# A graph network with a mixture of experts: the second product of a tile behind the first of the next, and the routing's exponentials first

## The chip, the cores and the metric

The kernel runs on one core of one Trainium2 chip. Its time is that of one execution on the device, in microseconds (us); of several runs the median counts. The engines are named as the profile names them: PE (TensorE, its weight loads apart as PEld), DVE (VectorE), ACT (ScalarE), POOL (GpSimd) and SP (SyncE), which here only issues DMAs.

## The reference

Four layers follow each other on 3125 nodes with 256 numbers each, each behind a layer norm and added to its input: a graph convolution over 50,000 edges, an attention over slices, a second, two-step graph convolution with PReLU, and a mixture of eight experts. Only the last one matters here:

```python
def _L1_ffn_ref(x, gate_w, gate_b, W1, b1, W2, b2):
    xf = x.reshape(-1, Dd)
    probs = jax.nn.softmax(xf @ gate_w + gate_b, axis=-1)
    top2_vals, top2_idx = jax.lax.top_k(probs, 2)
    cw = zeros((N, Ee)).at[arange(N)[:, None], top2_idx].add(top2_vals)
    def step(acc, params):
        w1, bb1, w2, bb2, we = params
        h = jax.nn.gelu(xf @ w1 + bb1, approximate=False)
        y = h @ w2 + bb2
        return (acc + we[:, None] * y, None)
    out, _ = jax.lax.scan(step, jnp.zeros_like(xf), (W1, b1, W2, b2, cw.T))
```

w1 is 256 x 512 and w2 512 x 256 for each expert, all in float32. Each node needs only its two chosen experts.

## The kernel before

The kernel is written without a scheduler: each engine has its own list of instructions, and semaphores order them across engines. What matters lies in the last block, the experts (from line 1985). There the rows that go to the same expert are collected into tiles. There are 39 of them (TILES). The first 13 (FULL = 13) are narrow, 128 rows each, and their plan is made from the first 1280 nodes only, so that they can begin early. The other 26 are planned from all nodes by a longer computation; of them two wide tiles of 256 rows are followed by one narrow tile, over and over, and tile 38 is narrow too. So tiles 13, 14, 16, 17, 19, 20 and so on are wide.

A tile n goes through these steps:

- POOL gathers its rows from memory, an indirect DMA for each 128 rows, together with their gates (gather, line 1966, recorded at 1967). There are four buffers for the rows of a tile, eight for the narrow tiles at the start.
- PE transposes the rows (turn, line 2346, recorded at 2353) into bank n % 2. This waits for the gather.
- The transposes are copied out of the bank (take): for tiles 0 to 12 by ACT (line 2246, recorded at 2250), from tile 13 on by DVE (line 2090, recorded at 2094).
- PE makes the first product (hidden, line 2357, recorded at 2365), in two halves into two banks. It waits for the copy and for the first weights of the tile's expert, which SP loads (512 KB, line 2544) into one of two buffers when the first product of tile n-2 is done.
- ACT applies the bias and the Gelu in four instructions (line 2333), after the second product of tile n-2 has let go of their buffer.
- PE makes the second product (line 2500); all second weights are in SBUF. In the texts it is called y(n).
- DVE adds the second bias and multiplies by the gate of each row (evict, line 2096, recorded at 2105 and 2108).
- POOL adds the result to the output in memory, by an indirect DMA with accumulation for each 128 rows (line 2615). The scatter of tile n waits until that of tile n-1 has landed, since two tiles can hold the same row.

The order of each engine is written out by hand. PE has turn(0), hidden(0), and then for each n hidden(n) (where n > 0), turn(n+1) and the second product of n (lines 2474 to 2503). ACT has for each n its four activations, then take(n+1); for n = 0 then the exponentials of the routing (lines 2322 to 2342), for which DVE waits at 2122. Exponential and Gelu need different tables in ACT, each of which is loaded when it isn't there. DVE interleaves the routing of all nodes with the evictions of tiles 0 to 9 (lines 2113 to 2236). Of this routing: the choices are ready at 2140 (e_dv 2), the gates at 2141 (e_dv 3); PE then sums the choices for tile 3 (line 2490) and their ranks ahead of the second product of tile 4 (line 2492), DVE copies the ranks at 2161; the one-hots of the places are at 2218 to 2223, and PE multiplies them at line 2468, ahead of the second product of tile 10; from that DVE makes the table of rows (line 2232, e_dv 6). From tile 10 on DVE has, for each n, take(n+1) (where n+1 is at least 13) and evict(n).

POOL (lines 2601 to 2621) waits for evict(n), then gathers: tile n+8 as long as that is under 13; tile n+4 for n = 9 to 12, ahead of the scatter of n, where n = 9 waits for the table of rows; and for n from 13 on tile n+4 behind the scatters of n. SP (lines 2537 to 2555) stores all rows and gates (1980 KB) between the weight loads of tiles 4 and 5, when the gates are ready.

Of the kernel before, what the change touches and what calls it, by code (L numbers as in the profile page):

```python
# [7 lines left out]
ALU, ACT, AX = mybir.AluOpType, mybir.ActivationFunctionType, mybir.AxisListType  # L8
# [27 lines left out]
FULL = -(-(2 * CA * P - X * (P - 1)) // P)  # L36
# [4 lines left out]
TILES = FULL + REST  # L41
# [44 lines left out]
def build(nc, x, src, dst, g0_w, g0_b, w_fx, b_fx, w_x, b_x, w_slice, b_slice, w_q, w_k, w_v,  # L86
# [3 lines left out]
    with ctx:  # L90
# [1611 lines left out]
        def table(m, w=NC * X):  # L1702
            return SR[:, m * NC * X:m * NC * X + w]
        lg, prob, one1, one2, tmp, pick, rank, slot = (
            table(m).rearrange("p (c e) -> p c e", e=X) for m in range(8))
# [266 lines left out]
        def expert_of(eng, n):  # L1972
            if n < FULL:
                return eng.value_load(ftile_i[0:1, n:n + 1], min_val=0, max_val=X - 1)
            return eng.value_load(tile_i[0:1, numbered(n):numbered(n) + 1], min_val=0, max_val=X - 1)
# [9 lines left out]
        with nc.Block() as block:  # L1985
            @block.vector
            def _(dve):
# [102 lines left out]
                def take(n):  # L2090
                    dve.wait_ge(x_tr.sem, n + 1)
                    dve.wait_ge(h_mm.sem, 2 * (n - 1))
                    w = KF * parts(n) * P
                    nc.vector.tensor_copy(xT[:, n % 2, 0:w], ps[n % 2][:, 0:w]).then_inc(x_cp.sem, 1)
# [140 lines left out]
                step(nc.vector.tensor_tensor(out_f, out_f, row_f, ALU.add))  # L2235
                step(nc.vector.tensor_copy(out_i, out_f))
                for n in range(10, TILES):
                    if FULL <= n + 1 < TILES:
                        take(n + 1)
                    evict(n)  # L2240

                ch.close(step.done)

            @block.scalar
            def _(act):
                def take(n):
                    act.wait_ge(x_tr.sem, n + 1)
                    if n >= 2:
                        act.wait_ge(h_mm.sem, 2 * (n - 1))
                    nc.scalar.copy(xT[:, n % 2, 0:F], ps[n % 2][:, 0:F]).then_inc(x_cp.sem, 1)  # L2250
# [71 lines left out]
                for n in range(TILES):  # L2322
                    if n == FULL:
                        act.wait_ge(e_dv.sem, 4)
                    b = n % 2
                    w = parts(n) * P
                    expert = expert_of(act, n)
                    if n >= 2:
                        act.wait_ge(y_mm.sem, n - 1)
                    for m in range(KH):  # L2330
                        if m % 2 == 0:
                            act.wait_ge(h_mm.sem, 2 * n + m // 2 + 1)
                        last = nc.scalar.activation(hT[:, b, m, 0:w],  # L2333
                                                    ps[2 + 2 * b + m // 2][:, (m % 2) * w:(m % 2 + 1) * w], ACT.Gelu,
                                                    bias=b1T[:, bass.ds(expert, 1), m:m + 1].rearrange("p a k -> p (a k)"))
                        if m % 2:
                            last.then_inc(h_ac.sem, 1)
                    if n + 1 < FULL:
                        take(n + 1)
                    if n == 0:  # L2340
                        act.wait_ge(e_dv.sem, 1)
                        nc.scalar.activation(prob, lg, ACT.Exp).then_inc(e_ac.sem, 1)

            @block.tensor
            def _(pe):
# [125 lines left out]

                pe.wait_ge(e_ld.sem, e_ld.at(16 * (KH + 1 + X)))

                for n in range(TILES):
                    b = n % 2
                    expert = expert_of(pe, n)

                    if n:
                        hidden(n)

                    if n + 1 < TILES:
                        turn(n + 1)

                    if n == 0:
                        pe.wait_ge(e_dv.sem, 1)
                    if n >= 2:
                        pe.wait_ge(y_ev.sem, n - 1)
                    if n == 3:
                        pe.wait_ge(e_dv.sem, 2)
                        nc.tensor.matmul(ps[7][:, F:F + NC * X], ones[:], picks, start=True, stop=True)  # L2490
                    if n == 4:
                        nc.tensor.matmul(ps[6][:, F:F + NC * X], before[:], picks, start=True, stop=True)
                    if n == 10:
                        places_of(0)
                        places_of(1)
                    for h in range(parts(n)):
                        for k in range(KH):
                            if h == 0 and k % 2 == 0:
                                pe.wait_ge(h_ac.sem, 2 * n + k // 2 + 1)
                            last = nc.tensor.matmul(ps[6 + b][:, h * F:(h + 1) * F], hT[:, b, k, h * P:(h + 1) * P],  # L2500
                                                    w2[:, k, bass.ds(expert, 1), :].rearrange("p a n -> p (a n)"),
                                                    start=(k == 0), stop=(k == KH - 1))
                    last.then_inc(y_mm.sem, 1)

            @block.sync
            def _(sp):
# [137 lines left out]
```

## Time and profile before

| what | us |
|---|---|
| median of 3 runs | 1302.27 |
| the three runs | 1302.27, 1302.09, 1312.83 |
| span of the profiled execution | 1300.2 |
| PE busy in it | 1227.5 |
| POOL busy in it | 200.3 |

The profiled execution's whole time isn't given apart from its span; by the median some 2.1 us lie around the span. The experts take the last quarter of it, from about 1050 us on. PE's rows in a timeline begin before the end of the row ahead, as matmuls are pipelined; the rows of the chain have this taken off. "<-" in a row names what ended the idle time in front of it. A float32 product is recorded as two matmuls, so that a first or second product of one tile has 16 records (8 for the second product of a narrow tile).

### The profile page before, as it was taken

What the parts mean: (1) busy time and instruction counts of PE and PEld (TensorE: products, weight loads), DVE (VectorE), ACT (ScalarE), POOL (GpSimd) and SP (SyncE); (2) the same over time, 40 slices, a digit from 0 to 9 for tenths busy, and PEclk for the clock granted to TensorE, in tenths of its full rate; (3) what the DMA queues carried; (4) which work ended last, traced back from release to release, by engine and by line L of the source; (5) the groups of instructions that cost most, each with busy time, mean ns of one, the idle gap of its engine ahead of it and who ended that gap; (6) DMA issues with size and microseconds to landing.
All of it is one profiled execution on the core that took longest, in us unless ns stands there. A gap on an engine that the chain in (4) does not pass through costs nothing.

```text
span 1300.2 us, 20280 instructions
## 1 busy us (share of the span) xinstructions
PE 1227.5 (94%) x7475; PEld 843.3 (65%) x7475; DVE 580.9 (45%) x1601; ACT 488.8 (38%) x1192; POOL 200.3 (15%) x205
## 2 busy tenths in 40 slices
PE   3599999989999999999999999999999989899996
PEld 2377777745557644457777644447777778788885
DVE  5968877567764511221333332231224656323231
ACT  5865666357743597760000000110212243222221
POOL 3000000023310000000000000000000043577664
PEclk8599999999999999999999999999999989999998
DMA  6133123310003055566556445569766657566663
GB/s 190 30 128 104 49 103 128 135 38 1 1 1 129 2 176 152 153 152 152 127 127 127 127 142 153 154 148 210 163 118 122 193 176 205 136 160 150 148 148 66
DMA packets 256968, 159.96 MB, mean 123 GB/s; under 512 B 172832, under 2 KB 243951, under 8 KB 256732
## 3 DMA queue, kind: packets, MB, share of 16 engines
q1 hardware_dynamic: 245788, 143.58, 40.2%
q0 software_dynamic: 11072, 14.97, 6.5%
q8 instruction: 64, 1.05, 0.3%
q14 instruction: 44, 0.36, 0.1%
HBM read 82.15 MB, written 36.35 MB: 91 GB/s over the span
## 4 chain that ended last, share of the span: by engine, by line
PE 61%; DVE 3%; DMA 3%; issue 1%; POOL 0%; ACT 0%; POOLq 0%; DVEq 0%; ACTq 0%
PE bank L1010 21%; PE bank L1024 21%; PE bank L2500 7%; PE bank L2365 6%; PE bank L1045 2%; PE bank L1655 2%; DMA out<-weights,first_places 2%; PE bank L2353 1%; PE bank L1907 1%; DVE bnbuf L824 0%; PE bank L1897 0%; DVE weights L2058 0%; DMA normed<-rows_and_gates,agg_in_out 0%; DVE tb L2023 0%; DMA out<-weights,agg_in_out 0%
## 5 line engine op out<-in xcount | busy, mean ns | idle before, releaser
L1010 PE MATMUL bank<-weights,agg_in_out 128*128 128x320 f16 x2000 | 274.8, 299 | 0.0
L1024 PE MATMUL bank<-weights 128*128 128x512 f16 x1250 | 271.1, 379 | 0.9 <-issue 0.8
L1010 PEld LDWEIGHTS bank<-weights,agg_in_out 128*128 128x128 f16 x2000 | 195.7, 98 | 76.2
L1024 PEld LDWEIGHTS bank<-weights 128*128 128x128 f16 x1250 | 121.8, 98 | 149.5 <-DVEq L2015 2.1
L1147 PE MATMUL bank<-weights,agg_in_out 128*128 128x320 f16 x1000 | 163.1, 299 | 1.6 <-ACT weights L543 1.6
L543 ACT CAST weights<-bank 128x500 f16<-128x500 f32 x160 | 114.1, 723 | 66.9 <-PE bank L532 66.9
L840 POOL TENSOR_TENSOR shift<-shift,rstd 128x5 f32<-128x5 f32 x15 | 3.7, 245 | 865.1 <-ACT rstd L845 865.1
L2333 ACT ACTIVATE weights<-bank,weights 128x128 f32<-128x128 f32 (+1 forms) x156 | 55.8, 411 | 163.1 <-PE bank L2365 125.5
L2500 PE MATMUL bank<-weights 128*128 x448 | 111.2, 396 | 3.0 <-ACT weights L2333 2.8
L1147 PEld LDWEIGHTS bank<-weights,agg_in_out 128*128 128x128 f16 x1000 | 91.6, 98 | 28.5 <-issue 2.3
L2365 PE MATMUL bank<-wk,weights 128*128 128x128 f32 (+1 forms) x624 | 106.6, 325 | 2.9 <-DMA weights<-in_L_ffn_W 2.7
L2013 DVE SCALAR_TENSOR_TENSOR wk<-bank,inverse_degree,wk 128x256 f32<-128x256 f32 x50 | 24.0, 480 | 182.2 <-ACT wk L2271 182.2
L2365 PEld LDWEIGHTS bank<-wk,weights 128*128 128x128 f32 x624 | 96.3, 196 | 12.7 <-DMA weights<-in_L_ffn_W 3.1
L2500 PEld LDWEIGHTS bank<-weights 128*128 128x128 f32 x448 | 83.2, 196 | 20.0 <-issue 10.3
L1055 ACT COPY agg_in_out<-bank 128x320 f32<-128x320 f32 x20 | 8.5, 427 | 213.7 <-PE bank L1010 213.7
L2271 ACT ACTIVATE wk<-bank,inverse_degree 128x256 f32<-128x256 f32 x50 | 23.6, 474 | 153.0 <-PE bank L1024 142.2
L522 DVE TENSOR_TENSOR wk<-iota,low_source 128x512 f16<-128x512 f16 x160 | 67.4, 421 | 28.6 <-PE bank L532 26.8
L532 PE MATMUL bank<-wn,wk 128*128 128x125 f16 x640 | 64.5, 227 | 13.7 <-DVE wn L523 12.6
L2615 POOL DMA_INDIRECT out<-weights,agg_in_out x43 | 68.4, 1590 | 42.4 <-DMA out<-weights,agg_in_out 23.9
L1063 DVE COPY agg_in_out<-bank 128x320 f32<-128x320 f32 x20 | 9.8, 491 | 140.1 <-PE bank L1010 120.1
L532 PEld LDWEIGHTS bank<-wn,wk 128*128 128x128 f16 x640 | 49.4, 101 | 29.2 <-DVE wn L523 17.3
L523 DVE TENSOR_TENSOR wn<-iota_quarters,row_of_edge 128x504 f16<-128x504 f16 x160 | 66.5, 416 | 0.0
(428 smaller groups left out, 1465.9 us busy)
## 6 DMA issues: line engine op xcount, KB each, us to landing
weights<-counts_source_target SPq DMA_DIRECT2D x50, 800.0 KB, 4.6
counts_source_target<-weights SPq DMA_DIRECT2D x5, 4000.0 KB, 14.0
weights<-in_L_ffn_W SPq DMA_DIRECT2D x39, 512.0 KB
weights<-in_L_ffn_W SPq DMA_DIRECT2D x4, 1024.0 KB, 5.6
residual<-in_x SPq DMA_DIRECT2D x4, 640.0 KB, 5.1
rows_and_gates<-normed SPq DMA_DIRECT2D x1, 1980.0 KB
out<-residual SPq DMA_DIRECT2D x1, 1792.0 KB
first_rows_and_gates<-normed SPq DMA_DIRECT2D x1, 1320.0 KB, 6.0
```

The costliest lines, as they stand in the source:

```text
L522: nc.vector.tensor_tensor(couples(ohs[:, u]), ramp(4, P), twins(slo2[:, g, :], P), ALU.is_equal)
L523: nc.vector.tensor_tensor(couples(ohr[:, u, :, 0:NR + 1]), quarter_ramp(4, NR + 1), twins(rk2[:, g, :], NR + 1), ALU.is_equal).then_inc(q_ ...
L532: last = nc.tensor.matmul(ps[QBANK[u]][:, t * NR:(t + 1) * NR], ohs[:, u, t, :], ohr[:, u, t, 0:NR], start=True, stop=True)
L543: nc.scalar.copy(to, ps[QBANK[q % 4]][:, 0:4 * NR].rearrange("p (t n c) -> p t c n", t=4, c=NC)).then_inc(q_ev.sem, 1)
L1010: last = nc.tensor.matmul(bank, source[:, 5 * k + c, part * F + fh * P:part * F + fh * P + P], MB[:, k, c, h * HALF:(h + 1) * HALF], start ...
L1024: last = nc.tensor.matmul(ps[j][:, :], MB[:, k, c, j * P:(j + 1) * P], source[:, 5 * k + c, :], start=(k == 0 and c == 0), stop=(k == 4 an ...
L1045: last = nc.tensor.matmul(ps[product_bank(n)][:, 0:F], aggT[:, k, c * P:(c + 1) * P], gw[:, kw, k, :], start=(k == 0), stop=(k == KF - 1))
L1147: last = nc.tensor.matmul(bank, XH2[:, c, part * F + fh * P:part * F + fh * P + P], ats[b % 2][:, c, h * HALF:(h + 1) * HALF], start=(m == ...
L2333: last = nc.scalar.activation(hT[:, b, m, 0:w], ps[2 + 2 * b + m // 2][:, (m % 2) * w:(m % 2 + 1) * w], ACT.Gelu, bias=b1T[:, bass.ds(expe ...
L2365: last = nc.tensor.matmul(ps[2 + 2 * b + m // 2][:, (m % 2) * w:(m % 2 + 1) * w], w1b[:, b, k, m * P:(m + 1) * P], xT[:, b, k * w:(k + 1) ...
L2500: last = nc.tensor.matmul(ps[6 + b][:, h * F:(h + 1) * F], hT[:, b, k, h * P:(h + 1) * P], w2[:, k, bass.ds(expert, 1), :].rearrange("p a ...
L2615: pool.indirect_dma_start(out=out, in_=results_at(n)[:, h, :], in_offset=None, out_offset=bass.IndirectOffsetOnAxis(ap=rows_of(n, h, out_i ...
```

## The change

On PE turn(1) comes first, and then for each n hidden(n+1), turn(n+2) and the second product of n. At the border (tile 12 to 13) this is taken back: hidden(13), turn(13) and turn(14) come behind the second product of tile 12, since tile 13 needs the plan of all nodes. On ACT the copy for tile 1 and the exponentials come first of all, and take(n+1) stands between the two halves of the activations of n for n = 1 to 11. On DVE take(n+2) comes ahead of evict(n) from n = 13 on; take(13) stands ahead of evict(12) and take(14) behind it. POOL and SP are as before.

```diff
@@ -2235,9 +2235,13 @@
                 for n in range(10, TILES):
-                    if FULL <= n + 1 < TILES:
-                        take(n + 1)
+                    if n == FULL - 1:
+                        take(FULL)
+                    if FULL + 2 <= n + 2 < TILES:
+                        take(n + 2)
                     evict(n)
+                    if n == FULL - 1:
+                        take(FULL + 1)
@@ -2325,9 +2329,15 @@
                     expert = expert_of(act, n)
+                    if n == 0:
+                        take(1)
+                        act.wait_ge(e_dv.sem, 1)
+                        nc.scalar.activation(prob, lg, ACT.Exp).then_inc(e_ac.sem, 1)
                     if n >= 2:
                         act.wait_ge(y_mm.sem, n - 1)
                     for m in range(KH):
+                        if m == 2 and 0 < n < FULL - 1:
+                            take(n + 1)
                         if m % 2 == 0:
                             act.wait_ge(h_mm.sem, 2 * n + m // 2 + 1)
...
-                    if n + 1 < FULL:
-                        take(n + 1)
-                    if n == 0:
-                        act.wait_ge(e_dv.sem, 1)
-                        nc.scalar.activation(prob, lg, ACT.Exp).then_inc(e_ac.sem, 1)
@@ -2471,15 +2476,15 @@
+                turn(1)
                 for n in range(TILES):
                     b = n % 2
                     expert = expert_of(pe, n)
 
-                    if n:
-                        hidden(n)
-
-                    if n + 1 < TILES:
-                        turn(n + 1)
+                    if n + 1 < TILES and n != FULL - 1:
+                        hidden(n + 1)
+                    if n + 2 < TILES and not FULL <= n + 2 <= FULL + 1:
+                        turn(n + 2)
@@ -2501,6 +2506,10 @@
                     last.then_inc(y_mm.sem, 1)
+                    if n == FULL - 1:
+                        turn(FULL)
+                        hidden(FULL)
+                        turn(FULL + 1)
```

## Rows read from the trace of the kernel before

**Rows 1.** The page, first part: busy us, share of span, instructions.

```profile
PE 1227.5 (94%) x7475; PEld 843.3 (65%) x7475; DVE 580.9 (45%) x1601; ACT 488.8 (38%) x1192; POOL 200.3 (15%) x205
```

**Rows 2.** Busy time by stretch; after the five engines: clock, DMA share, GB/s.

```profile
1050.00:1100.00 50.00, 44.17 (x269) 39.02 (x268) 25.14 (x95) 21.58 (x57) 18.28 (x18) 0.89 0.67 197
...
1200.00:1250.00 50.00, 49.94 (x257) 43.15 (x256) 13.91 (x30) 12.07 (x31) 35.23 (x27) 1.00 0.65 150
```

**Rows 3.** Chain of waits, one round: start us, length us, what.

```profile
1148.51 3.53 PE bank L2500 x16
1152.05 3.45 PE bank L2365 x16
1155.72 0.86 PE bank L2500 x4
1156.61 2.85 PE bank L2500 x12
1159.46 1.78 PE bank L2365 x16
1161.69 1.74 PE bank L2500 x8
...
1167.31 3.53 PE bank L2500 x16
```

**Rows 4.** Timelines of PE, ACT and DVE, tiles 0 and 1.

```profile
1058.74 3.77 PE L2500 MATMUL bank<-weights 128*128 x8 [1.53 <-ACT weights L2333]
...
1066.41 1.99 PE L2500 MATMUL bank<-weights 128*128 x8 [1.04 <-ACT weights L2333]
...
1059.29 1.28 ACT L2342 ACT_TABLE_LOAD   x1
...
1064.35 1.28 ACT L2333 ACT_TABLE_LOAD   x1 [3.39 <-PE bank L2365]
...
1068.57 0.42 DVE L2105 TENSOR_TENSOR weights<-bank,weights 128x256 f32<-128x256 f32 x1 [2.07 <-PE bank L2500]
```

**Rows 5.** Timelines of PE and DVE around tiles 4 and 5.

```profile
1079.08 1.89 PE L2500 MATMUL bank<-weights 128*128 x8
1083.67 2.91 PE L2365 MATMUL bank<-wk,weights 128*128 128x128 f32 x16 [2.69 <-DMA weights<-in_L_ffn_W]
...
1081.92 0.37 DVE L2161 COPY agg_in_out<-bank 128x200 f32<-128x200 f32 x1
...
1089.47 0.43 DVE L2105 TENSOR_TENSOR weights<-bank,weights 128x256 f32<-128x256 f32 x1 [2.53 <-PE bank L2500]
```

**Rows 6.** Tiles 12 to 14: timelines of PE and DVE, then chain of waits.

```profile
1121.73 0.71 PE L2353 MATMUL bank<-ident,normed 128*128 128x128 f32 x4 [2.11 <-DMA normed<-rows_and_gates,agg_in_out]
...
1129.73 0.69 DVE L2094 COPY wk<-bank 128x512 f32<-128x512 f32 x1 [2.84 <-PE bank L2353]
...
1116.88 4.81 DMA normed<-rows_and_gates,agg_in_out
...
1122.45 3.36 PE bank L2500 x8
```

**Rows 7.** Timeline of POOL behind tile 16's second product.

```profile
1154.61 1.62 POOL L2615 DMA_INDIRECT out<-weights,agg_in_out  x1 [0.30 <-issue]
...
1158.41 1.08 POOL L1967 DMA_INDIRECT normed<-rows_and_gates,agg_in_out  x1 [0.30 <-issue]
1159.80 1.05 POOL L1967 DMA_INDIRECT normed<-rows_and_gates,agg_in_out  x1 [0.30 <-issue]
```

**Rows 8.** Chain of waits, the end.

```profile
1287.94 3.79 DMA out<-weights,agg_in_out
```

**Rows 9.** DMA engines' busy tenths, 1151 to 1158 in 40 slices.

```profile
DMA  9940003100000057560000396420000029332997
```

**Rows 10.** Busy time by stretch around two gaps of PE.

```profile
1081.00:1089.00 8.00, 5.33 (x26) 4.96 (x27) 4.51 (x21) 1.52 (x5) 3.09 (x3) 0.79 0.70 210
...
1106.00:1114.00 8.00, 6.16 (x72) 5.77 (x71) 5.01 (x9) 1.51 (x5) 3.11 (x2) 1.00 0.42 124
```

## The prediction

> **What bounds the kernel now.** I read the page's first part, then the table by stretches, then the chain of waits from 1050 us on, then the timeline of each engine there. TensorE is busy for 94% of the span [rows 1], and the edit touches only what follows about 1057 us, so the question is how near to full the expert stage is and what fills the rest. Two stretches differ [rows 2]: from 1050 to 1100 TensorE is busy 44 of 50 us with VectorE at 25, from 1200 to 1250 it is busy 49.94 of 50.
>
> In the second stretch (tiles 13 to 38, in the pattern wide, wide, narrow) the chain is TensorE alone [rows 3]. A wide tile costs 3.45 us for the first product (x16, line 2365) and 3.53 for the second (line 2500), a narrow one 1.78 and 1.74. Between a first and a second product stand the transposes of the next tile: 0.22 us for two, 0.45 for four. From the end of tile 16's second product (1152.04) to the end of tile 19's (1170.84) one round of three tiles takes 18.8 us. Only one real wait is in it: the split into 0.86 + 2.85 of a second product behind a narrow tile's transposes, some 0.2 us late on the activations. The whole edit can take 0.2 us a round out of this stretch.
>
> In the first stretch (tiles 0 to 12, narrow) VectorE makes the routing tables between the evictions, and the gather of tile 13 waits for it. TensorE has three gaps there: 1.04 us ahead of tile 1's second product [rows 4], 2.69 us ahead of tile 5's first product, where the weights of tile 5 come behind the 1980 KB store of rows and gates [rows 5], and 2.1 us at tile 13's transposes, for its gather [rows 6].
>
> **The sum's base.** The profile's span is 1300.2 us and the median of the timed runs 1302.27, so 2.1 us lie around the span. Differences are worked out in the span and put on the median. A measurement of this kernel can tell about 1% (13 us) from no change.
>
> **Part 1, the exponentials ahead of tile 0's activations.** Before: Gelu table, four activations, a copy, a table load of 1.28 us, the exponential; then another load of 1.28 at tile 1 [rows 4]. After: copy, load, exponential, load, activations. One load of 1.28 us goes, and VectorE gets its exponentials about that much sooner. But tile 0's second product, which began at 1058.74, now has the copy, a load (1.28) and the exponential ahead of its activations, and the copy waits for tile 1's transposes: some 3 us later. Meanwhile TensorE does the first product of tile 1. VectorE then waits for tile 1's second product, which ended at 1068.24 and whose eviction at 1068.57 cost it 2.07 us of waiting [rows 4]. I put that product's end at 1068.6, so the 1.3 us are eaten and the routing goes on 0 to 0.5 us late. Bounds: 1.3 us sooner to 1.5 later. I take 0.3 later.
>
> **Part 2, the shifted order in tiles 1 to 12.** With weights in time the order changes nothing, as each activation gets more cover. The exception is tile 5. Its weights are queued on SP behind the store of rows and gates, which waits for VectorE's gates (about 1073), and land at 1083.6 whatever TensorE does. Before, the second product of tile 4 came ahead of this wait and ended at 1080.97; VectorE read its ranks at 1081.92 [rows 5]. Now hidden(5) and turn(6) (first product and transposes) stand ahead of y(4) (second product). TensorE runs dry after y(3), near 1077, and waits some 7 us instead of 2.7; then come the first product (2.9 us, at the lower clock, as in the row of before), transposes, ranks and y(4), ending at 89 to 90. VectorE's copy of the ranks moves from 1081.9 to about 1089.5. It had waited 2.53 us in front of tile 5's eviction at 1089.47 [rows 5], which it gets back in part: the 5.0 us of steps between copy and eviction start late, and evict(5) comes at about 1095.5. The routing is then 6 us late and stays so, since from there VectorE works without a wait for TensorE. Bounds: 4 us (if the gates come 1.3 us sooner) to 8.
>
> How much reaches tile 13? The second of its two gathers began at 1116.88 and landed 4.81 us later [rows 6]. Now it begins near 1123 and lands between 1126 and 1128, and turn(13) starts near 1127.4 instead of 1121.73. In return y(12), which took 3.36 us at the lower clock behind turn(13) before [rows 6], is now done ahead of it, for nothing. Before, hidden(13) began at 1125.8. Now it begins after turn(13) (0.45) and VectorE's copy (0.69 by the row of tile 14's [rows 6], with both hand-overs an estimated 0.95), at 1128.8, and hidden(14) waits for its own copy again, 0.95, as no second product stands between. Sum at the border: 3.0 + 0.95 = +4.0 us. Bounds: +1 (no delay of the routing) to +7.
>
> **Part 3, the wide stretch: the gather gets less time.** POOL's order is unchanged: after evict(n) it scatters tile n, then gathers tile n+4. Turn(n+4) needs that gather. Before, hidden(n+1) to hidden(n+3), y(n+1), y(n+2) and two turns lay between y(n) and turn(n+4). In the new order hidden(n+2), turn(n+3), y(n+1) and hidden(n+3) are all: one product of each kind and one turn less. Take tile 16 [rows 3, 7]: Its second product ended at 1152.04, its scatters began at 1154.61 (2.57 later: eviction by VectorE, semaphores, POOL just free), its two gathers for tile 20 ended on POOL at 1160.85. So 8.8 us pass before the gather is even sent. To land: the last scatter of the run landed 3.79 us after its start, of which POOL took 1.55, so 2.2 after [rows 8]; tile 13's gather 3.8 after, behind weight loads [rows 6]; and the DMA view of 1151 to 1158 shows the engines busy until about 1155.5 after the gather that POOL finished at 1154.3, so at least 1.2 [rows 9]. I take 2.1, nearest to the scatter's row and to the quiet view.
>
> Now the loop over one round: y(16) ends; 2.57 + 6.24 + 2.1 = 10.9 to the landing; turn(20) 0.45; y(18) 1.74; hidden(20) 3.45; turn(21) 0.22; y(19) 3.53. Sum 20.3 us, against 18.8 that TensorE needs now. The leg of TensorE in it is 9.4, so the gather would have to be there in 9.4 us and takes 10.9. TensorE waits 1.5 to 1.7 us before turn(17), 20, 23 and so on, once a round. The other two gathers of a round have room as soon as this one has stretched it. POOL's own work, 5 scatters at 1.9 and 5 gathers at 1.4 with the waits for landings, is near 17.9 and does not bind. From tile 17 to tile 38 there are 7 rounds: 7 x 1.5 = +10.5 us. Bounds by landing: 1.2 gives +4, 3.8 gives +22.
>
> The Trainium skill ("DMA: Bandwidth & Descriptors", Anatomy of one DMA — SWDGE (gpsimd) path) gives a fixed 2.0 us and the bytes over 436e3 a microsecond; for 128 rows of 264 floats that is an estimate of 2.3 us, and the loop would be 20.5 and the part +12. By the row of tile 13's gather it would be +22. No row of before shows a gather's landing in the quiet stretch.
>
> **Part 4, the tail.** The end is set by the scatters of tiles 37 and 38 behind y(37). Hidden(38) now stands ahead of y(37): +1.8 us.
>
> Sum: 4.0 + 10.5 + 1.8 = +16.3, thus 1302.3 + 16.3 = 1318.6; I say 1318.
>
> **Rivals.**
> A (0.5): the forecast, 1310 to 1324.
> B (0.2): the gather lands fast, 1.2 us after POOL, or the routing loses nothing. The loop is 19.4, 7 x 0.6 = +4, border +2 to 4, tail 1.8: about +9, 1310 or a little below. For it: the quiet view of rows 9. Against: the scatter's 2.2.
> C (0.2): the waits make the clock fall. Around the 2.7 us gap of tile 5 the mean granted clock was 0.79 and the next products took 2.9 instead of 2.0 us; around the 1.84 us gap at 1109 it stayed at 1.00 [rows 10]. A gap of 1.6 is below that, hence the small chance. A fall costs about 1.7 us (tile 12's product: 3.36 for 1.74), in the loop, 7 times: +12, 1330. The Trainium skill ("TensorE: Matmul & The Clock Gate", HAM oscillation — how this bites in real kernels) tells of kernels in which a wait in every pass throttles the array each time; by it the time would be this 1330.
> D (0.1): not slower. The scatters and gathers keep up: the landing is hidden because POOL starts earlier than 2.57 us after the product. It decides at 9.4 us from y(n) to the landing. Then the 0.2 us waits go (8 x 0.2), y(12) covers 1.7 of the gather's wait and the exponentials give 1.3: -4.6, 1298. Against: the 8.8 us already spent on POOL's rows leave 0.6 for a landing, and no row shows one so short. More than 1% faster would need 13 us, while all gaps of TensorE in the stage together are about 9.
>
> Chances: over 1% slower (above 1315.3) is most of A and all of C, 0.58; within 1% the rest of A, B and D, 0.38; faster by over 1% 0.04. Range 1304 to 1331.
>
> **What would show it.** Right: TensorE's row at line 2353 waits 1.5 us once a round "<- DMA normed"; busy in 1200 to 1250 falls from 49.9 to about 46; rounds of 20.3 us; a 7 us gap at line 2365 near 1077 to 1084; the eviction of tile 5 near 1095; two table loads after 1056 us instead of three. Wrong: rounds of 18.6 with no wait at line 2353; evict(5) still near 1089; or a granted clock below 0.95 in 1150 to 1250, which is rival C.

## The result: slower by 1.3%, and the profile after

The changed kernel takes 1324.38 us (median of 6 runs, 1323.08 to 1327.81) where the kernel before, run beside it, takes 1305.4 (6 runs, 1302.09 to 1312.83). The medians lie 19.0 us apart. The ratio is 1.0127, with a 95% interval of 1.0099 to 1.0156: slower by 1.0 to 1.6%, or 16.6 us by the ratio. I had forecast 1318, in a range of 1304 to 1331, with slower by over 1% at 0.58. The spans of the two profiled executions, 1300.2 and 1321.7 us, lie 21.5 us apart. That is more than the 16.6 us of the ratio, since the profiled execution of before was among its fastest.

The page of the changed kernel, its span and first part, has the work unchanged, against [rows 1]:

```profile
span 1321.7 us, 20280 instructions
...
PE 1225.7 (93%) x7475; PEld 844.7 (64%) x7475; DVE 581.7 (44%) x1601; ACT 486.8 (37%) x1191; POOL 200.1 (15%) x205
```

The table of busy time by stretch answers to [rows 2]:

```profile
1050.00:1100.00 50.00, 40.44 (x257) 37.69 (x257) 20.01 (x76) 18.70 (x52) 15.77 (x13) 0.85 0.67 191
...
1200.00:1250.00 50.00, 46.60 (x247) 40.27 (x246) 13.05 (x27) 12.13 (x32) 31.38 (x24) 1.00 0.58 137
```

TensorE, busy 49.94 us of the stretch from 1200 to 1250 before, has 46.60 now, with the clock still at 1.00. In the first stretch it falls from 44.17 to 40.44, and there the mean granted clock falls from 0.89 to 0.85 (its two levels are 2.4 and 1.2 GHz, 1.00 and 0.5). POOL, busy 35.23 us from 1200 on, has 31.38, the same work in longer rounds.

**The wide stretch.** The chain of waits of the changed kernel, one round from tile 16's second product to the transposes of tile 20, and on to those of tile 23 (start us, length us, what):

```profile
1160.75 3.47 PE bank L2505 x16
...
1166.65 0.36 POOL out L2624
...
1168.57 1.56 POOL out L2624
...
1170.44 1.07 POOL normed L1967
...
1171.82 3.41 DMA normed<-rows_and_gates,agg_in_out
1175.28 0.66 PE bank L2358 x4
1175.93 1.73 PE bank L2505 x8
1177.66 3.45 PE bank L2370 x16
...
1181.34 3.47 PE bank L2505 x16
...
1195.89 0.66 PE bank L2358 x4
```

In [rows 3] this was TensorE alone. Now the chain leaves it. The second product ends at 1164.22, two scatters start at 1166.65 and 1168.57, two gathers follow, the second of which starts at 1171.82, and 3.41 us later its rows are there, 2.4 after POOL is done with it. Only then do tile 20's transposes run, and behind them 1.73, 3.45, 0.22 and 3.47 us of TensorE. From 1175.28 to 1195.89 a round takes 20.6 us, where it took 18.8. From the product's end to the landing it is 11.0 us, and TensorE had work for 9.2 of them.

From 1216 us on the waits are mostly spread over two transposes of a round, 0.2 to 1.2 us each, and the chain also goes over landings of scatters. This one is tile 27's:

```profile
1241.93 6.08 DMA out<-weights,agg_in_out
```

Tile 28's scatters wait for it on POOL, and the gather of tile 32 stands behind them. The rounds stay at 20.0 to 20.9 us.

**Tiles 4 and 5.** The timelines of PE and DVE of the changed kernel, against [rows 5]:

```profile
1073.54 1.89 PE L2505 MATMUL bank<-weights 128*128 x8
1083.80 3.78 PE L2370 MATMUL bank<-wk,weights 128*128 128x128 f32 x16 [8.37 <-DMA weights<-in_L_ffn_W]
...
1088.46 2.18 PE L2505 MATMUL bank<-weights 128*128 x8
...
1090.74 0.37 DVE L2161 COPY agg_in_out<-bank 128x200 f32<-128x200 f32 x1 [9.97 <-PE bank L2505]
...
1096.87 0.42 DVE L2105 TENSOR_TENSOR weights<-bank,weights 128x256 f32<-128x256 f32 x1 [0.86 <-issue]
```

Tile 3's second product is done at 1075.4, then TensorE waits 8.37 us for tile 5's weights; the second product of tile 4 runs behind that, at 1088.46 instead of 1079.08. VectorE copies the ranks at 1090.74 instead of 1081.92 and evicts tile 5 at 1096.87 instead of 1089.47.

**The border.** The timeline of PE at tiles 13 and 14, against [rows 6]:

```profile
1128.95 0.66 PE L2358 MATMUL bank<-ident,normed 128*128 128x128 f32 x4 [2.09 <-DMA normed<-rows_and_gates,agg_in_out]
1130.43 5.16 PE L2370 MATMUL bank<-wk,weights 128*128 128x256 f32 x16 [0.83 <-issue]
...
1136.86 3.69 PE L2370 MATMUL bank<-wk,weights 128*128 128x256 f32 x16 [0.83 <-issue]
...
1140.61 3.62 PE L2505 MATMUL bank<-weights 128*128 x16
```

The transposes of tile 13 start 7.2 us later than before. Each of the two first products waits 0.83 us; VectorE's copy (0.69 us, the first from 1129.64 on) ends 0.1 us before the first of them starts. The first of them takes 5.16 us instead of 3.45 at full clock. When it and the second product of tile 13 and the first of tile 14 are done (1140.77 + 3.47 = 1144.24) the kernel before stood at 1136.90 (the start of tile 14's second product, behind 1133.23 + 3.45 + 0.22, in its chain).

### The profile page after: what moved, and what is told of

Its sections match the earlier page's. It is cut to its first block, busy times and chain, and to the rows that moved or that the text cites. A ratio compares the mean times of both kernels' runs of the same rounds, so it can differ in the third digit from the quotient of the medians.

```text
span 1321.7 us, 20280 instructions
## 1 busy us (share of the span) xinstructions
PE 1225.7 (93%) x7475; PEld 844.7 (64%) x7475; DVE 581.7 (44%) x1601; ACT 486.8 (37%) x1191; POOL 200.1 (15%) x205
## 4 chain that ended last, share of the span: by engine, by line
PE 53%; DVE 5%; DMA 4%; issue 4%; POOL 2%; DVEq 0%; POOLq 0%; ACT 0%; SPq 0%; ACTq 0%
PE bank L1010 21%; PE bank L1024 20%; PE bank L2505 3%; PE bank L2370 3%; PE bank L1045 2%; PE bank L1655 2%; DMA normed<-rows_and_gates,agg_in_out 2%; DMA out<-weights,agg_in_out 1%; POOL out L2624 1%; PE bank L1907 1%; DMA weights<-in_L_ffn_W 1%; POOL normed L1967 1%; DVE weights L2105 1%; PE bank L2358 1%; PE bank L1897 0%
## 5 line engine op out<-in xcount | busy, mean ns | idle before, releaser
L2370 PE MATMUL bank<-wk,weights 128*128 128x128 f32 (+1 forms) x624 | 110.3, 333 | 11.0 <-DMA weights<-in_L_ffn_W 8.4
L2370 PEld LDWEIGHTS bank<-wk,weights 128*128 128x128 f32 x624 | 99.4, 202 | 20.7 <-DMA weights<-in_L_ffn_W 8.8
L2505 PE MATMUL bank<-weights 128*128 x448 | 103.6, 381 | 1.1 <-DVE weights L2108 1.1
```

Source lines behind the costliest of these rows:

```text
L2370: last = nc.tensor.matmul(ps[2 + 2 * b + m // 2][:, (m % 2) * w:(m % 2 + 1) * w], w1b[:, b, k, m * P:(m + 1) * P], xT[:, b, k * w:(k + 1) ...
```

## The experiments

Ratios are to the kernel before, which ran beside each group on the same chip; its median was 1307 to 1309 us in those. The groups ran on different chips, so runs of two groups are compared by their ratios.

### The gathers ahead of the scatters

```diff
-                    if FULL <= n + 4 < FULL + 4:
+                    if FULL <= n + 4 < TILES:
                         gather(pool, n + 4)
...
-                    if FULL + 4 <= n + 4 < TILES:
-                        gather(pool, n + 4)
```

> The changed kernel with one edit on POOL: from tile 13 on the gather of tile n+4 comes ahead of the scatters of tile n instead of behind them, so it is sent some 3.8 us sooner; nothing else moves. My theory (the wide stretch loses because the gather of tile n+4 has 9.4 us where it takes 10.9 to 11.3): the loop over a round falls from 20.6 to under 18.6, TensorE's waits at the transposes in the wide stretch vanish, and the time falls by 10 to 13 us against the changed kernel, to 5 to 9 us above the kernel before. Rival 1 (the loss comes from VectorE's copies standing ahead of the evictions, or from the order on TensorE itself): the waits stay or move to the products and the time stays within 3 us of the changed kernel, 19 us above the one before. Rival 2 (POOL as a whole is the bound): nothing is gained either, as its sum of work is the same.

Measured: 1311.4 us, ratio 1.0038 [1.0015, 1.0062], so 5 us above the kernel before and 12 below the changed one by the ratios. In the first rounds the chain of waits of this run is TensorE's alone again:

```profile
1140.34 3.46 PE bank L2505 x16
1143.79 1.78 PE bank L2370 x16
...
1146.01 3.46 PE bank L2505 x16
1149.47 3.45 PE bank L2370 x16
...
1158.76 3.46 PE bank L2505 x16
```

From 1140.34 to 1158.76, wide tile to the same wide tile of the next round, it takes 18.4 us, 0.4 less than before: the product behind a narrow tile's transposes is in one piece of 3.46 us now, where [rows 3] had it split into 0.86 and 2.85. From 1125 us on TensorE's transposes wait for gathers 2.4 us in all, against 13.6 in the changed kernel. All the extra rounds' time hangs on when POOL sends the gather. The rivals fall: VectorE's copies and TensorE's order are as in the changed kernel, and so is the sum of POOL's work. What stays is the border: tile 13's second product ends at 1143.80, 6.9 us behind the same work before. From 1240 us on the chain goes over POOL's scatters and their landings, a bound that comes back below.

### Part 1 alone: the exponentials first

```diff
                     expert = expert_of(act, n)
+                    if n == 0:
+                        take(1)
+                        act.wait_ge(e_dv.sem, 1)
+                        nc.scalar.activation(prob, lg, ACT.Exp).then_inc(e_ac.sem, 1)
...
-                    if n + 1 < FULL:
+                    if 0 < n < FULL - 1:
                         take(n + 1)
-                    if n == 0:
-                        act.wait_ge(e_dv.sem, 1)
-                        nc.scalar.activation(prob, lg, ACT.Exp).then_inc(e_ac.sem, 1)
```

> The kernel before with part 1 alone: on ScalarE the copy for tile 1 and the exponentials stand ahead of tile 0's activations; TensorE, VectorE and POOL keep their old order. My theory (one table load goes, VectorE then waits for the second product of tile 1 anyway, so nothing of it arrives): within 2 us of the kernel before, the choices ready at 1072 to 1074 us. Rival (the routing's chain carries the gain through to tile 13's gather): 1.3 us or more faster, all later routing steps sooner by that much.

Measured: 1308.79 us, ratio 1.0012 [0.9988, 1.0037]: no difference. The timeline of DVE in this run:

```profile
1059.32 0.36 DVE L2122 TENSOR_REDUCE agg_in_out<-agg_in_out 128x25 f32<-128x200 f32 x1 [0.43 <-ACT agg_in_out L2331]
...
1065.49 0.42 DVE L2105 TENSOR_TENSOR weights<-bank,weights 128x256 f32<-128x256 f32 x1 [4.75 <-PE bank L2501]
...
1073.90 0.28 DVE L2141 TENSOR_TENSOR normed<-agg_in_out 128x120 f32<-128x120 f32 x1
```

The exponentials arrive at 1059.32 (1060.99 before). Then VectorE waits 4.75 us for tile 0's second product, evicts at 1065.49 what it evicted at 1063.28, and has the gates 1.1 us later than before (1073.90 against 1072.77). In the changed kernel the earlier exponentials look so, in the timelines of ACT and then DVE:

```profile
1058.30 0.37 ACT L2335 ACTIVATE agg_in_out<-agg_in_out 128x200 f32<-128x200 f32 x1 [0.16 <-DVE agg_in_out L2119]
1058.69 1.28 ACT L2343 ACT_TABLE_LOAD   x1
...
1064.13 0.42 DVE L2105 TENSOR_TENSOR weights<-bank,weights 128x256 f32<-128x256 f32 x1 [4.01 <-PE bank L2505]
...
1068.15 0.42 DVE L2105 TENSOR_TENSOR weights<-bank,weights 128x256 f32<-128x256 f32 x1 [0.80 <-PE bank L2505]
```

The exponential at 1058.30, one load behind it, evictions of tiles 0 and 1 at 1064.13 and 1068.15 against 1063.28 and 1068.57 [rows 4]: an even trade.

This run has the old order in the wide stretch, and yet its profile shows the transposes there waiting for gathers in three places (timeline of PE):

```profile
1149.40 0.65 PE L2354 MATMUL bank<-ident,normed 128*128 128x128 f32 x4 [1.97 <-DMA normed<-rows_and_gates,agg_in_out]
...
1169.48 0.66 PE L2354 MATMUL bank<-ident,normed 128*128 128x128 f32 x4 [1.14 <-DMA normed<-rows_and_gates,agg_in_out]
...
1209.80 1.11 PE L2354 MATMUL bank<-ident,normed 128*128 128x128 f32 x4 [2.48 <-DMA normed<-rows_and_gates,agg_in_out]
```

So the old order too has single late gathers in some executions; the profile of before happened to hold none. That may be why the times of the kernel before spread over some 10 us; it is not shown.

### The shift in the narrow tiles alone, and in the wide ones alone

The first run has the changed kernel's order up to tile 12 and the old one behind it, on PE (DVE likewise):

```diff
-                    if n + 1 < TILES and n != FULL - 1:
-                        hidden(n + 1)
-                    if n + 2 < TILES and not FULL <= n + 2 <= FULL + 1:
-                        turn(n + 2)
+                    if n < FULL - 1:
+                        hidden(n + 1)
+                        if n + 2 < FULL:
+                            turn(n + 2)
+                    if n >= FULL:
+                        hidden(n)
+                        if n + 1 < TILES:
+                            turn(n + 1)
...
                     if n == FULL - 1:
                         turn(FULL)
-                        hidden(FULL)
-                        turn(FULL + 1)
```

> The changed kernel in tiles 0 to 12, exponentials included, and the order of before from tile 13 on (turn(13) stays behind the second product of tile 12). My theory (the ranks and the second product of tile 4 sit behind the late weights of tile 5; routing 7 us late, part of it covered by the second product of tile 12): 4 to 8 us slower than before; VectorE's copy of the ranks near 1090; rounds of 18.8 us in the wide stretch and no wait at its transposes but the first. Rival (the narrow part is harmless and all of the loss is in the wide one): within 1 us of the kernel before.

Measured: 1313.47 us, ratio 1.0056 [1.0036, 1.0076], +7.3 us. VectorE copies the ranks at 1090.73, and the table of rows is ready at 1123.67 instead of 1114.39.

The second run is the other half: old order and old exponentials up to tile 12, the new order from the border on (PE is shown, DVE likewise).

```diff
-                    if n:
-                        hidden(n)
-                    if n + 1 < TILES:
-                        turn(n + 1)
+                    if 0 < n < FULL:
+                        hidden(n)
+                    if n + 1 < FULL:
+                        turn(n + 1)
+                    if FULL <= n < TILES - 1:
+                        hidden(n + 1)
+                        if n + 2 < TILES:
+                            turn(n + 2)
...
+                    if n == FULL - 1:
+                        turn(FULL)
+                        hidden(FULL)
+                        turn(FULL + 1)
```

> The kernel before in tiles 0 to 12, exponentials included, and the new order from tile 12's second product on. My theory: the copy of the ranks stays near 1082, the border costs -2 to +1 us (the second product of tile 12 covers part of the gather's wait, two copies are uncovered), the rounds grow from 18.8 to 20.6, 7 of them +12 to 13, and the tail +1.8: 12 to 16 us slower than before. Together with the run that shifts the narrow tiles alone it should give the 19 us of the whole. Rival (the wide stretch suffers only from the late start behind the narrow tiles): under 6 us slower.

Measured: 1319.49 us, ratio 1.0077 [1.0041, 1.0113], +10 us by the ratio, a little under the 12 to 16 that I expected. Its timeline of PE has the border early and then the same waits:

```profile
1121.86 3.69 PE L2369 MATMUL bank<-wk,weights 128*128 128x256 f32 x16 [0.83 <-issue]
...
1151.66 1.11 PE L2357 MATMUL bank<-ident,normed 128*128 128x128 f32 x4 [6.65 <-DMA normed<-rows_and_gates,agg_in_out]
...
1196.11 0.66 PE L2357 MATMUL bank<-ident,normed 128*128 128x128 f32 x4 [2.25 <-DMA normed<-rows_and_gates,agg_in_out]
```

The first product of tile 13 starts at 1121.86, 4 us sooner than before, and the gain is lost at once: tile 17's transposes wait 6.65 us, since POOL, which waited for the landing of tile 12's scatter, began tile 13's only at 1143.70 and with it the gathers behind. The two halves give 1.0056 and 1.0077, together 1.33% where the whole measured 1.27%. Both parts of the change cost, and within their intervals they add up.

### The store behind the weights of tile 5

```diff
-                    if n == 4:
+                    if n == 5:
                         sp.wait_ge(e_dv.sem, 3)
                         sp.dma_start(zg_dram[CA * P:NP, ...
```

> The changed kernel with one edit on SP: the store of the 1980 KB of rows and gates is issued behind the first weights of tile 5 instead of ahead of them. My theory (the ranks are late because they sit behind the product that waits for these weights): the gap of 8.4 us moves from tile 5's first product to tile 6's, the ranks and the second product of tile 4 come on time, VectorE copies the ranks at 1081 to 1083 instead of 1091 and makes the table of rows 6 to 8 us sooner (near 1115); the wide rounds stay at 20.6 us. Time 5 to 8 us below the changed kernel, 11 to 14 above the one before. Rival (the border is late because of the border's own order, two uncovered copies and the lower clock, and not because of the routing): at most 2 us below the changed kernel.

Measured: 1319.07 us (4 runs), ratio 1.0107 [1.0067, 1.0146]. That is 2.6 us below the changed kernel by the ratios, where I had expected 5 to 8. The interval reaches over that of the changed kernel, so by time alone the run decides nothing, and the rival (at most 2 us) isn't excluded. Its span is 1314.0 against 1321.7, and the timelines of PE and DVE show the step itself:

```profile
1083.93 3.78 PE L2370 MATMUL bank<-wk,weights 128*128 128x128 f32 x16 [4.26 <-DMA weights<-in_L_ffn_W]
...
1080.96 0.37 DVE L2161 COPY agg_in_out<-bank 128x200 f32<-128x200 f32 x1
...
1115.51 0.19 DVE L2232 CAST agg_in_out<-agg_in_out 128x44 int32<-128x44 f32 x1
```

The gap is half as long and stands in front of tile 6's weights now. The ranks are copied at 1080.96 instead of 1090.74, the table of rows is ready at 1115.51 instead of 1121.92. That the product of tile 5 held the ranks is shown by the rows; its price in time this run leaves open, and the run with the narrow shift alone tells it better.

### Both cures, in the new order and in the old

The gathers ahead of the scatters as above, and the store in five parts (POOL then waits for all five, 80 instead of 16 on their semaphore):

```diff
-                    if n == 4:
-                        sp.wait_ge(e_dv.sem, 3)
-                        sp.dma_start(zg_dram[CA * P:NP, ...
+                    if 5 <= n < 10:
+                        if n == 5:
+                            sp.wait_ge(e_dv.sem, 3)
+                        c = CA + 3 * (n - 5)
+                        sp.dma_start(zg_dram[c * P:(c + 3) * P, ...
```

> The changed kernel with the gathers of tile n+4 ahead of the scatters of tile n (from tile 13 on), and with the store of rows and gates in five parts of 384 rows, one behind the weights of each of the tiles 5 to 9. My theory: no wait at the transposes in the wide rounds, and no gap over 3 us in tiles 5 to 9, so the routing is ready 7 to 10 us sooner than in the changed kernel; 1298 to 1304 us in a run where the kernel before has 1305, so 1 to 5 us faster than before; what is left against it is two uncovered copies at the border and 1.8 us of tail. Rival (both prices share one cause, and taking one away leaves the other to take its place): no better than the gather first alone, 5 us slower than before.

Measured: 1304.93 us, ratio 1.0001 [0.9977, 1.0026]. All of the loss is gone, and nothing is won, where I had expected 1 to 5 us. VectorE's timeline and POOL's say why:

```profile
1111.89 0.19 DVE L2232 CAST agg_in_out<-agg_in_out 128x44 int32<-128x44 f32 x1
...
1110.29 1.56 POOL L2626 DMA_INDIRECT out<-weights,first_places  x1 [3.16 <-DVE weights L2108]
1116.03 1.56 POOL L2626 DMA_INDIRECT out<-weights,first_places  x1 [4.19 <-DMA out<-weights,first_places]
1117.89 1.08 POOL L1967 DMA_INDIRECT normed<-rows_and_gates,agg_in_out  x1 [0.30 <-issue]
```

The table of rows was ready at 1111.89, 10 us sooner than in the changed kernel and 2.5 sooner than in the kernel before. But POOL has the scatter of tile 8 in front of the gather of tile 13, and that scatter waits until the one before has landed, 4.91 us after its start. The gather left at 1117.89, and the transposes of tile 13 waited 5.4 us, until 1122.24; before they started at 1121.73.

> The kernel before with the gathers of tile n+4 ahead of the scatters of tile n, from tile 13 on. In its own profile no wait of the wide stretch falls on a gather, in two runs of the same order there were such waits of 1 to 2.5 us. My theory (the old order leaves the gather 3 to 5 us of slack, so the edit can only take away the few late ones): 0 to 3 us faster than before, rounds of 18.8. Rival (sending the gathers first delays the scatters and so the evictions, which cost the changed kernel with this edit its remaining 5 us): 2 to 5 us slower.

The kernel before with only the gathers first: 1307.51 us, ratio 1.0001 [0.9979, 1.0022]. No difference; the old order doesn't need it. Its chain of waits from 1120 us on now has 37% in the landings of scatters (2% before), so the gathers sent first push the scatters back.

> The kernel before with both edits: gathers ahead of scatters from tile 13 on, and the store in five parts behind the weights of tiles 5 to 9. My theory: the gap of 2.7 us at tile 5 goes, VectorE loses its wait of 2.5 us ahead of tile 5's eviction, and the table of rows is ready about 2 us sooner: 2 to 5 us faster than before, and as fast as or faster than the changed kernel with the same edits by the 1.8 us of the tail. Rival (the new order is worth more once its gathers and its store are out of the way): the changed kernel with both edits is the faster of the two by over 2 us.

The kernel before with both edits: 1307.13 us, ratio 1.0004 [0.9982, 1.0026]. The routing was 1.9 us sooner (1112.53), tile 13's transposes came at 1122.18, no sooner than before: no gain, where I had expected 2 to 5 us. Between the two orders with both edits there is no difference that was measured.

### The gather of tile 13 ahead of the scatter of tile 8

```diff
-                    if n == FULL - 4:
+                    if n == FULL - 5:
+                        pool.wait_ge(y_ev.sem, n + 2)
                         pool.wait_ge(e_st.sem, 80)
                         pool.wait_ge(e_dv.sem, 6)
-                    if FULL <= n + 4 < TILES:
+                        gather(pool, FULL)
+                    if FULL < n + 4 < TILES:
                         gather(pool, n + 4)
```

The diff is against the runs with both edits. The new waits for the eviction of tile 9 and for the table of rows stand ahead of the scatter of tile 8 too.

> The kernel before (old order) with the gathers ahead of the scatters, the store in five parts, and on POOL the gather of tile 13 ahead of the scatter of tile 8 instead of behind it. In the runs with the first two edits the table of rows was ready at 1112 but POOL stood in front of the scatter of tile 8 until the one of tile 7 had landed, and sent the gathers of tile 13 only at 1118. My theory: they now go out at about 1113, TensorE's wait of 4.4 us at tile 13's transposes falls under 1 us: 2 to 5 us faster than before. Rival (tile 13 is held by the DMA queues, busy with weights, and not by POOL's order): the transposes of tile 13 stay at 1122 and the time within 1 us of before.

Old order: 1309.87 us, ratio 1.0011 [0.9988, 1.0034]. The gather leaves at 1114.06 and its transposes start at 1120.16, 2 us sooner than in the run with both edits, but the time doesn't follow. My expectation was wrong. The timelines of PE and then DVE at tile 37 say what took the place:

```profile
1279.25 3.91 PE L2500 MATMUL bank<-weights 128*128 x16
...
1286.29 0.69 DVE L2105 TENSOR_TENSOR weights<-bank,weights 128x512 f32<-128x512 f32 x1 [5.14 <-DMA out<-weights,agg_in_out]
```

TensorE is done with tile 37 at 1283.2, half a microsecond sooner than before (1283.7), but the eviction waits until a scatter has landed and so begins at 1286.29, and the last scatter leaves at 1296.84 instead of 1292.56. In this profile the chain of scatters, each behind the landing of the one before, sets the end and not TensorE.

> The changed kernel (new order, exponentials first) with the same three edits. My theory: the wait of 5.4 us at tile 13's transposes falls to 1 to 2 us, and the wide stretch has neither the waits for gathers nor the 0.2 us a round for activations: 3 to 6 us faster than before, within 1.5 us of the old order with the same edits, as two uncovered copies and the tail (3.5 us) stand against 0.2 us a round and the cover of tile 13's gather. Rival (the new order itself costs, whatever its gathers do): 3 us or more slower than the old order with the same edits.

New order: 1313.16 us, ratio 1.0031 [1.0012, 1.005]: slower than the kernel before, where I had expected it 3 to 6 us faster. By the ratios it is 4 us above the run without the edit, with intervals that overlap, and 2.6 us above the old order with the same edits, which neither shows nor excludes the rival that the new order itself costs 3 us. The timeline of PE:

```profile
1118.80 0.66 PE L2358 MATMUL bank<-ident,normed 128*128 128x128 f32 x4 [0.96 <-DMA normed<-rows_and_gates,agg_in_out]
...
1128.88 0.96 PE L2358 MATMUL bank<-ident,normed 128*128 128x128 f32 x4 [4.90 <-DMA normed<-rows_and_gates,agg_in_out]
1130.67 6.29 PE L2370 MATMUL bank<-wk,weights 128*128 128x256 f32 x16 [0.83 <-DVE wk L2094]
```

Tile 13's transposes run at 1118.80, and the wait has only moved on to tile 14's, 4.90 us, because its gather stands behind the next scatter. The lull there then costs a first product of 6.29 us.

The last run has, besides, the first product of tile 38 behind the second product of tile 37:

```diff
-                    if n + 1 < TILES and n != FULL - 1:
+                    if n + 1 < TILES and n not in (FULL - 1, TILES - 2):
                         hidden(n + 1)
...
+                    if n == TILES - 2:
+                        hidden(TILES - 1)
```

> The run before this one with one more edit on TensorE: the first product of tile 38 stands behind the second product of tile 37 again. It measures the tail alone. My theory (the end is set by the scatters behind the second product of tile 37, which the first product of tile 38 delays by its 1.78 us): 1.5 to 2 us faster than the run without the edit. Rival (the end hangs on tile 38 or on the scatter of tile 36): no difference, or slower.

Measured: 1312.85 us, ratio 1.0026 [1.0008, 1.0044], no difference from the run without it, where I had expected 1.5 to 2 us. The chain of waits of this run shows that it could not measure the tail:

```profile
1290.22 2.69 DMA out<-weights,agg_in_out
...
1293.75 1.55 POOL out L2630
```

The scatter of tile 37 starts once that of tile 36 has landed (1290.22 + 2.69 = 1292.91), and in the run without the edit it is the same (1288.52 + 2.70 = 1291.22, then 1292.05). In both runs the end hangs on the scatters, as the rival had it, and not on the second product of tile 37. For the changed kernel itself the tail stays a reading of its profile.

No version beat the kernel before.

## Why the prediction was right, and what was mis-sized

The mechanism, its places and the sign came out as written. The spans lie 21.5 us apart where the sum had 16.3; the ratio's interval stands for 13 to 20 us. By the rows it is 7.3 at the border, 12.3 in the loop and 1.8 at the end, 21.4 in all.

- **Part 1** (0.3 us later): nothing measurable, as predicted; the gates came at 1072.31 in the changed kernel, 0.5 us sooner than before. That tile 0's second product would wait until 1061.7 came out at 1062.00; the evictions behind it lost as much as the exponentials had gained.
- **Part 2, the ranks:** right in kind. I had TensorE dry at 1077 for 7 us; it was dry at 1075.4 for 8.37. The ranks were forecast for 1089.5 and came at 1090.74, evict(5) for 1095.5 and came at 1096.87. The routing was 7.4 us late at evict(5) and 7.5 at the table of rows (1121.92 against 1114.39), not 6.
- **Part 2, the border** (+4.0): this is the term that was mis-sized most. At equal work the profile has 1144.24 against 1136.90, +7.3 us, of which 0.4 was there before the experts began. I had the gather landing between 1126 and 1128 and hidden(13) starting at 1128.8. It started at 1130.43, at the lower clock, which took 1.7 us more. I had counted the lower clock of the old y(12) as saved and none for what follows the new gap.
- **Part 3, the loop** (+10.5): 2.57 + 6.24 + 2.1 = 10.9 us to the landing was forecast and is 11.0 in the rows; the round of 20.3 is 20.6, and 20.4 on the mean from turn(17) at 1154.69 to turn(38) at 1297.68 (143.0 over 7 rounds). From 1144.24 to y(37)'s end, less the tail, the stretch takes 12.3 us more than before. The run with the gathers first gives 12 us by the ratios. Two sentences of the forecast were wrong in the later rounds: that the other gathers of a round have room, and that POOL's work with its waits for landings doesn't bind. From 1216 us on the chain goes over scatters of 4.77, 4.35 and 6.08 us to their landing, and tiles 28, 31 and 32 wait as well. That the rounds came out near 20.3 all the same, through another part of the loop, was luck. The row of 3.79 us was read as the last scatter of the run; it is the second of tile 37.
- **Part 4, the tail** (+1.8): the chain's end has it as forecast, hidden(38) in front of y(37), and then the scatters. No run confirms its size, since in the last two the end hangs on the landings of the scatters.

```profile
1299.88 1.78 PE bank L2370 x16
1301.66 3.47 PE bank L2505 x16
...
1309.37 3.85 DMA out<-weights,agg_in_out
```

- **Rival B** (a landing of 1.2 us): false, it was 2.4 in the row above. The Trainium skill's fit ("DMA: Bandwidth & Descriptors", Anatomy of one DMA — SWDGE (gpsimd) path), an estimate of 2.3 us for 128 rows, is near this if it is counted from the end of POOL's instruction; from its start the row has 3.41.
- **Rival C** (the clock falls in the loop): false. The waits, 1.9 us at most, left the clock at 1.00 from 1150 to 1300. It did fall behind the wait of 8.37 us (0.50 from 1083.8 to 1088) and behind those of 2.09 and 0.83 (0.70 from 1130.4 to 1135.4). The kernel of which the Trainium skill tells ("TensorE: Matmul & The Clock Gate", HAM oscillation — how this bites in real kernels) has longer waits in each pass than these, so it should not have been carried over to 1330 us, and these rows don't contradict it.
- **Rival D** (the gather keeps up): false for the change as made. Its arithmetic for the rounds was right for another kernel: with the gathers first they are 18.4 us, and the 0.2 us waits are gone.

What had not been seen ahead is what stands next in line. With both cures the routing of all nodes was ready 2.5 us sooner than in the kernel before, without any gain, as the scatters on POOL, each behind the landing of the one before, held tile 13's gather; and in most profiles with the gathers first the same chain of scatters set the end.

## What to carry to other kernels

When a step is moved ahead of another on one engine, write down for each thing it waits for how long the producer takes from its own start signal, and compare that with what is left between the two; here 11.0 us met 9.2, and no busy share showed it: POOL was busy for 15% of the span. A step that may wait for a transfer should not be put in front of one that somebody else is waiting for: the first product of tile 5 waited for weights that came no sooner, and took the routing with it. Taking a wait away shows its worth only when what stands next in line has room.

## What the runs showed of the hardware

The same first product of a wide tile took 3.45 us at 2.4 GHz. With a part of it at the lower level, 1.2 GHz, it took 5.16 behind gaps of 2.09 and 0.83 us, and 6.29 behind gaps of 4.90 and 0.83.

Waits of up to 1.9 us, one or two in most rounds of 20 us, left the granted clock at 1.00 over 150 us. The length of the gap alone doesn't decide: the wait of 2.25 us in the wide shift alone left the clock at 1.00 (1196 to 1208), the one of 2.11 us at tile 13 before [rows 6] was followed by 0.58 (1121.7 to 1125.8).

The second gather of 128 rows landed 2.4 us after POOL had finished issuing it in the round shown, and 1.8 to 2.9 after in other rounds of the changed kernel. The scatters with accumulation varied more. From the start of POOL's instruction, of which 1.55 us are POOL's, they landed 2.70 us later (tile 36, near the end of the runs with the gathers first), 3.85 (the second of tile 37), 4.91 (tile 7) and 6.08 (tile 27). What makes the difference is not shown.
